# Down products in split 16-bit pairs: a two-FFN and attention kernel on one Trainium2 core

## What is computed

```
x = x + 0.5 * ffn(layernorm(x));  x = x + attn(layernorm(x));  x = x + 0.5 * ffn(layernorm(x))
ffn(x):  scores = sigmoid(x @ router.T); 4 of 16 experts per token, from the best 2 of 4 groups
         h_e = silu(x @ gate_e.T) * (x @ up_e.T)             # 256 -> 128
         y   = sum over chosen e of w_e * (h_e @ down_e.T)   # 128 -> 256
         y  += silu(x @ sh_gate.T) * (x @ sh_up.T) @ sh_down.T   # two shared experts of 128
attn(x): q, k = softplus(gelu(x @ w1.T + b1) @ w2.T + b2); v, g = gelu(x @ w.T + b)
         linear attention over 16 heads (k.T q first), then * z * g, then @ p_w.T + p_b
```

## Time and profile before

| | us |
|---|---|
| median of three runs | 1950.2 |
| the profiled execution | 1945.92 |
| its span, first to last instruction | 1944.2 |
| TensorE busy | 1629.1 (84%) |
| TensorE weight loads | 1253.8 (64%) |
| GpSimd busy | 1115.1 (57%) |
| VectorE busy | 1031.3 (53%) |
| ScalarE busy | 923.8 (48%) |
| mean granted clock of TensorE | 0.943 of 2.4 GHz |

### The profile page before, as it was taken

The page is one execution under the profiler, slowest core; times in us unless marked ns, Lnnn a source line. Parts: engine busy times, 40 slices in busy tenths (PEclk is TensorE's granted clock), DMA queues, the critical chain, the costliest instruction groups (busy, mean ns, idle before and its releaser), DMA issues.

```text
span 1944.2 us, 36213 instructions
## 1 busy us (share of the span) xinstructions
PE 1629.1 (84%) x11159; PEld 1253.8 (64%) x11159; DVE 1031.3 (53%) x3186; ACT 923.8 (48%) x1435; POOL 1115.1 (57%) x1249
## 2 busy tenths in 40 slices
PE   5679999979989999999999999996999998887100
PEld 4447776757777777777777777774777676665100
DVE  4775747634455456557547456556646655232323
ACT  5334443424666556565665656654656642232000
POOL 2677757777033644554454564465466677454676
PEclk9889999999999999999999999999999999999555
DMA  9839998999646855775785785663598799999453
GB/s 311 323 133 249 262 246 245 257 252 258 156 112 168 211 139 146 199 202 146 196 197 153 173 216 155 168 188 87 123 240 212 200 258 289 254 259 296 133 164 118
DMA packets 586145, 393.48 MB, mean 202 GB/s; under 512 B 396375, under 2 KB 547054, under 8 KB 585966
## 3 DMA queue, kind: packets, MB, share of 16 engines
q1 hardware_dynamic: 536626, 256.85, 53.6%
q0 software_dynamic: 49152, 134.28, 22.7%
q10 hardware_dynamic: 188, 0.03, 0.0%
HBM read 101.61 MB, written 197.13 MB: 154 GB/s over the span
## 4 chain that ended last, share of the span: by engine, by line
PE 47%; POOL 20%; DVE 11%; issue 10%; SPq 5%; DMA 5%; ACT 3%; POOLq 0%; DVEq 0%; ACTq 0%
POOL xd L1320 11%; PE bank L993 10%; POOL yg L1334 8%; PE bank L848 6%; PE bank L850 6%; PE bank L849 6%; PE bank L1035 5%; SPq L829 3%; PE bank L997 3%; DVE xb L1547 2%; DMA yg<-yd,idx 2%; DMA xtp<-xd 2%; PE bank L1096 2%; PE bank L937 2%; PE bank L938 2%
## 5 line engine op out<-in xcount | busy, mean ns | idle before, releaser
L1320 POOL DMA_INDIRECT xd<-xs,idx x512 | 517.5, 1011 | 421.9 <-DVE picked L1471 216.4
L1334 POOL DMA_INDIRECT yg<-yd,idx x512 | 505.7, 988 | 231.4 <-issue 152.3
L993 PE MATMUL bank<-dn,h 128*128 x1408 | 377.6, 392 | 57.8 <-ACT ybuf L1190 26.9
L848 PE MATMUL bank<-xtp,gu_hi 128*128 128x256 f16 x1408 | 387.4, 275 | 28.9 <-DMA xtp<-xd 13.5
L1190 ACT ACTIVATE ybuf<-bank 128x512 f32<-128x512 f32 x352 | 209.5, 595 | 389.8 <-PE bank L993 381.4
L849 PE MATMUL bank<-xtp,gu_hi 128*128 128x256 f16 x1408 | 387.0, 275 | 0.0
L850 PE MATMUL bank<-xtp,gu_lo 128*128 128x256 f16 x1408 | 386.8, 275 | 0.0
L1522 DVE SCALAR_TENSOR_TENSOR h<-bank,h 128x512 f32<-128x512 f32 x240 | 165.6, 690 | 321.5 <-PE bank L850 265.5
L993 PEld LDWEIGHTS bank<-dn,h 128*128 128x128 f32 x1408 | 251.3, 194 | 111.5 <-issue 77.9
L1547 DVE SCALAR_TENSOR_TENSOR xb<-yg,comb,xb 128x256 f32<-128x256 f32 x512 | 208.2, 478 | 164.7 <-DMA yg<-yd,idx 164.6
L1183 ACT ACTIVATE h<-bank 128x512 f32<-128x512 f32 x240 | 141.6, 595 | 215.0 <-PE bank L850 126.3
(11 more groups left out here) (191 smaller groups left out, 2527.5 us busy)
## 6 DMA issues: line engine op xcount, KB each, us to landing
yd<-ybuf SPq DMA_DIRECT2D x352, 256.0 KB
xr<-xb SPq DMA_DIRECT2D x32, 512.0 KB, 4.7
xb<-xr SPq DMA_DIRECT2D x32, 512.0 KB
xd<-yg SPq DMA_DIRECT2D x3, 4096.0 KB, 14.6
xb<-in_attn_x_dram SPq DMA_DIRECT2D x16, 512.0 KB
xd<-xs,idx POOLq DMA_INDIRECT x512
yg<-yd,idx POOLq DMA_INDIRECT x512
out_dram<-xb SPq DMA_DIRECT2D x16, 512.0 KB, 3.3
```

Source lines behind the costliest of these rows:

```text
L848: pe.matmul(out_ap, a_hi, b_hi, start=(i == 0), stop=False)
L993: last = pe.matmul(dst, h[:, g % RING_H, c], w, start=True, stop=True)
L1320: pool.indirect_dma_start(out=xd[q % NC][:, :], out_offset=bass.IndirectOffsetOnAxis(ap=idx[:, r % SEQS, t, k:k + 1], axis=0), in_=xs[:, r ...
L1334: pool.indirect_dma_start(out=yg[:, half, t % 2, j].bitcast(U32), out_offset=None, in_=yd[q % NC][:, :], in_offset=bass.IndirectOffsetOnAx ...
```

## The change

The down products are made of 16-bit pairs, as gate and up are, three products each. For that the down weights are split when they are loaded (`dn_hi`, `dn_lo`), and h is split in every unit: silu writes a float32 buffer `m32` (a ring of two), prod multiplies in place with a scale of 8, a new ScalarE piece `h_hi` copies it to 16 bits, a new VectorE piece `h_lo` subtracts, and down waits for `h_lo`. The factor 8 is taken out in the weights of the experts and in the shared sum. The y ring shrinks from eight to seven. The two bias matmuls of the output projection become one, with the high part of the bias in row 0 and the low part in row 32 of one tile. The plan's weights follow: down 0.69 for 0.89, out 4.0 for 4.4, and 0.62 and 0.69 for the two new pieces.

```diff
-RING_Y = 8
+RING_Y = 7
 RING_H = 3
+RING_M = 2
+H_SCALE = 8.0
...
-        ... down=0.89, ... out=4.4),
+        ... down=0.69, ... out=4.0),
+        ACT: h_hi=0.62   DVE: h_lo=0.69   RANK: h_hi=0, h_lo=0
...
-        piece("silu", g, ("gate", g), *[freed] * (g >= RING_H))
+        piece("silu", g, ("gate", g), *[("h_lo", g - RING_M)] * (g >= RING_M))
         piece("prod", g, ("up", g), ("silu", g))
+        piece("h_hi", g, ("prod", g), *[freed] * (g >= RING_H))
+        piece("h_lo", g, ("h_hi", g))
-            piece("down", (g, b), ("prod", g), *before, *[("down", (g, 0))] * b)
+            piece("down", (g, b), ("h_lo", g), *before, *[("down", (g, 0))] * b)
...
-        split = [kind in ("gu", "at") for kind, _ in groups]
+        split = [kind in ("gu", "at", "dn") for kind, _ in groups]
-        dn = sb("dn", [P, NE, D])
+        dn_hi = sb("dn_hi", [P, NE, D], F16)
+        dn_lo = sb("dn_lo", [P, NE, D], F16)
-        h = sb("h", [P, RING_H, TOK])
+        m32 = sb("m32", [P, RING_M, TOK])
+        h = sb("h", [P, RING_H, 2, TOK], F16)
...
             def down(key):
-                pe.wait_ge(prod_done, g + 1)
+                pe.wait_ge(h_lo_done, g + 1)
-                        last = pe.matmul(dst, h[:, g % RING_H, c], w, start=True, stop=True)
+                        last = three(dst, [(h[:, g % RING_H, 0, c], h[:, g % RING_H, 1, c], w_hi, w_lo)])
...
-                    pe.matmul(dst, row0_16[:], pb_hi[:], start=False, stop=False)
-                    last = pe.matmul(dst, row0_16[:], pb_lo[:], start=False, stop=True)
+                    last = pe.matmul(dst, rows16[:], pb[:], start=False, stop=True)
...
             def silu(g):
                 act.wait_ge(gate_done, g + 1)
-                if g >= RING_H:
-                    act.wait_ge(down_done, nth(*plan.h_freed_by[g - RING_H]) + 1)
-                act.activation(h[:, g % RING_H], gate_ps[g % GATES][:], ACT.Silu, scale=INV_W).then_inc(silu_done, 1)
+                if g >= RING_M:
+                    act.wait_ge(h_lo_done, g - RING_M + 1)
+                act.activation(m32[:, g % RING_M], gate_ps[g % GATES][:], ACT.Silu, scale=INV_W).then_inc(silu_done, 1)
+            def h_hi(g):
+                act.wait_ge(prod_done, g + 1)
+                if g >= RING_H:
+                    act.wait_ge(down_done, nth(*plan.h_freed_by[g - RING_H]) + 1)
+                act.activation(h[:, g % RING_H, 0], m32[:, g % RING_M], ACT.Copy).then_inc(h_hi_done, 1)
...
+            def h_lo(g):
+                dve.wait_ge(h_hi_done, g + 1)
+                dve.tensor_tensor(h[:, g % RING_H, 1], m32[:, g % RING_M], h[:, g % RING_H, 0], ALU.subtract).then_inc(h_lo_done, 1)
```

More of the change, by code:

```diff
@@ L57 @@
 TABLE_STEPS = 14
-CONSTS = 29
+CONSTS = 30
 def stages():
@@ L81 @@
         SP=dict(wload=0.5, load=0.5, store=0.5, zero_rows=1.0, xload=2.6, ystore=0.5),
-        PE=dict(turn_w=0.5, small=0.4, turnR=0.95, logits=0.75, rank=0.25, turn_tab=0.3, gate=1.36, up=1.36, down=0.89,
-                turnA=0.95, proj=2.65, second=3.5, gproj=1.36, kv=1.85, z=0.5, apply=1.85, regroup=0.95, out=4.4),
+        PE=dict(turn_w=0.5, small=0.4, turnR=0.95, logits=0.75, rank=0.25, turn_tab=0.3, gate=1.36, up=1.36, down=0.69,
+                turnA=0.95, proj=2.65, second=3.5, gproj=1.36, kv=1.85, z=0.5, apply=1.85, regroup=0.95, out=4.0),
         ACT=dict(small_hi=0.6, w_hi=0.6, w_copy=0.6, norm=2.1, normA=2.1, xs_hi=1.05, xtf_hi=1.03, xtf_lo=1.03, sigmoid=0.9,
-                 silu=0.62, yev=0.62, xta_hi=1.2, gelu=2.0, absolute=1.05, exp=2.1, ln=2.1, gate_gelu=1.9, ot=1.6),
+                 silu=0.62, h_hi=0.62, yev=0.62, xta_hi=1.2, gelu=2.0, absolute=1.05, exp=2.1, ln=2.1, gate_gelu=1.9, ot=1.6),
         POOL=dict(rootR=1.7, rootA=1.7, scatter=5.1, gather=5.1),
         DVE=dict(small_lo=0.6, w_lo=0.69, group_p=0.5, stats=1.85, xs_lo=1.25, scores=0.8, groups=1.85, experts=2.3,
-                 slots=1.5, weights=2.2, table_cols=3.7, table=0.3, prod=0.7, shared_sum=0.7, combine=3.3,
+                 slots=1.5, weights=2.2, table_cols=3.7, table=0.3, prod=0.7, h_lo=0.69, shared_sum=0.7, combine=3.3,
                  statsA=1.85, xta_lo=1.4, add_bias=1.4, gate_bias=0.7, finish=1.25,
@@ L92 @@
     TABLE = dict(sigmoid=("exp", "gelu", "silu"), silu=("silu",), gelu=("gelu",), gate_gelu=("gelu",), exp=("exp",), ln=("ln",))
-    RANK = dict(down=0, silu=0, yev=0, prod=0, rootR=0, rootA=0)
+    RANK = dict(down=0, silu=0, yev=0, prod=0, h_hi=0, h_lo=0, rootR=0, rootA=0)
     EARLY = ("stats", "norm", "xs_hi", "xs_lo", "turnR", "xtf_hi", "xtf_lo", "logits", "sigmoid", "scores", "groups",
@@ L309, in unit_for @@
         r, p = self.next_shared, self.next_pair
-        if r < 2 * SEQS and ("xtf_lo", r) in self.ended and ("xtf_hi", r) in self.ended and ("w_copy", 2) in self.ended:
-            best = max(at, self.ended["xtf_lo", r], self.ended["xtf_hi", r], self.ended["w_copy", 2]), ("shared", r, 0)
-        if p < self.pairs and ("xload", p) in self.ended and ("w_copy", self.n_ffn - 1) in self.ended:
-            start = max(at, self.ended["xload", p], self.ended["w_copy", self.n_ffn - 1])
+        if r < 2 * SEQS and ("xtf_lo", r) in self.ended and ("xtf_hi", r) in self.ended and ("w_lo", 2) in self.ended:
+            best = max(at, self.ended["xtf_lo", r], self.ended["xtf_hi", r], self.ended["w_lo", 2]), ("shared", r, 0)
+        if p < self.pairs and ("xload", p) in self.ended and ("w_lo", self.n_ffn - 1) in self.ended:
+            start = max(at, self.ended["xload", p], self.ended["w_lo", self.n_ffn - 1])
             if best is None or start < best[0]:
@@ L766, in _ @@
                 sp.dma_start(row_bias[:, i, :], b.partition_broadcast(P)).then_inc(rows_loaded, 16)
-            sp.dma_start(pb_row, p_b.rearrange("(o d) -> o d", o=1)).then_inc(rows_loaded, 16)
+            for row in pb_rows:
+                sp.dma_start(row, p_b.rearrange("(o d) -> o d", o=1)).then_inc(rows_loaded, 16)
             def wload(n):
@@ L991, in down @@
                         c = slice(b * SLOT + j * P, b * SLOT + (j + 1) * P)
-                        w = dn[:, bass.ds(e, 1), :].rearrange("p e o -> p (e o)")
-                        last = pe.matmul(dst, h[:, g % RING_H, c], w, start=True, stop=True)
+                        w_hi, w_lo = (w[:, bass.ds(e, 1), :].rearrange("p e o -> p (e o)") for w in (dn_hi, dn_lo))
+                        last = three(dst, [(h[:, g % RING_H, 0, c], h[:, g % RING_H, 1, c], w_hi, w_lo)])
                     else:
                         c = slice((2 * b + j) * P, (2 * b + j + 1) * P)
-                        for s in range(SHARED):
-                            last = pe.matmul(dst, h[:, (g - 1 + s) % RING_H, c], dn[:, E + s, :],
-                                             start=(s == 0), stop=(s == SHARED - 1))
+                        parts = [h[:, (g - 1 + s) % RING_H] for s in range(SHARED)]
+                        last = three(dst, [(part[:, 0, c], part[:, 1, c], dn_hi[:, E + s], dn_lo[:, E + s])
+                                           for s, part in enumerate(parts)])
                 last.then_inc(down_done, 1)
@@ L1241, in _ @@
             plan.walk(dict(small_hi=small_hi, w_hi=w_hi, w_copy=w_copy, norm=norm, normA=normA, xs_hi=xs_hi, xtf_hi=xtf_hi,
-                           xtf_lo=xtf_lo, sigmoid=sigmoid, silu=silu, yev=yev, xta_hi=xta_hi, gelu=gelu,
+                           xtf_lo=xtf_lo, sigmoid=sigmoid, silu=silu, h_hi=h_hi, yev=yev, xta_hi=xta_hi, gelu=gelu,
                            absolute=absolute, exp=exp, ln=ln, gate_gelu=gate_gelu, ot=ot_))
@@ L1617, in _ @@
                            scores=scores_, groups=groups_, experts=experts_, slots=slots_, weights=weights_,
-                           table_cols=table_cols, table=table, prod=prod, shared_sum=shared_sum, combine=combine,
+                           table_cols=table_cols, table=table, prod=prod, h_lo=h_lo, shared_sum=shared_sum, combine=combine,
                            add_bias=add_bias, gate_bias=gate_bias, finish=finish_kq, kv_mask=kv_mask, mix=mix,
```

43 lines of the change are left out of this document (24 added, 19 removed).

## The result

The changed kernel takes 1962.6 us (median of 20 runs, 1954.0 to 1976.4), the kernel before 1949.8 (20 runs, 1938.4 to 1960.8). The ratio is **1.0067** with an interval of [1.0047, 1.0087]: 13 us slower, where 1918 us and a gain were forecast. The profiled execution has a span of 1958.1 us, before it was 1944.2.

What follows compares the result with a forecast made beforehand. The prediction took TensorE to bound the kernel between 420 and 1600: 67.1 us saved, less 16 for waits, 9 for GpSimd and 10 at the end, is 32.1, so the median of 1950.2 becomes 1918 us, range 1868 to 1968.

Steps and rivals of the forecast that it cites:

- a cheaper down product pays between 420 and 1600: In 420:1600, where TensorE was taken to set the pace, less down and bias work saves 67.1 us.
- The price of a down: On TensorE, a routed down falls from 0.87 us to 0.66 us, as six 16-bit matmuls.
- The first rival: Attention sequences, 70 us apart, set the pace and TensorE's saving turns idle: 1950 to 1960 us, no change; chance 0.17.
- The sign that the prediction set for it: In the attention stages: the same 70 us between applies, with TensorE busy for less, would show the forecast wrong.
- GpSimd: In 150:420, VectorE's new subtraction holds up scatters: 9 us lost, bounds 0 to 26.
- The passes: Splitting h adds 144 us of work on ScalarE and 166 on VectorE; both have room, so no cost was counted.
- The waits on the pair: TensorE's 23 waits in 420:1600 grow by up to 1.4 us each: between 0 and 32 us, 16 taken.
- The ends: First 150 us: 0 taken, between -16 and +7; last group: combines and gathers slip behind the last pairs, 10 us lost.
- The bias matmul and the y buffers: One bias matmul less in each of 64 cases saves TensorE 7.0 us; seven y buffers cost 0, bounds 0 and 7.1.
- a move by more than 20 us: Last stretch: a shift that large would show the forecast wrong and be the plan's new order, no engine's cost.

Runs made afterwards that it cites:

- e3: Changed kernel's operations without the split of h (the high part stands in for the low), in the order of the kernel before: 1938.8 us, 0.9935 of before.
- e12: Changed operations without the split of h, in exactly the order of e11: 1871.7 us, 0.9593 of the kernel before.
- e13: Changed operations without the split of h, in an order with head starts chosen for them: 1862.3 us, 0.9538 of the kernel before.
- e2: Changed kernel's order, with float32 downs and no split of h, one bias matmul and seven y buffers: 2002.6 us, 1.0266 of the kernel before.
- e6: Changed kernel in its own order, without the split of h and with five h buffers: 1942.7 us, 0.9973 of the kernel before.
- e4: As e3, in the order of the kernel before, but one product per down in place of three: 1922.1 us, 0.9846 of the kernel before.
- e7: As e6, in the changed kernel's order, but both splitting passes run and no down waits for them: 1962.1 us, 1.0072 of the kernel before.
- e10: All operations of the changed kernel, in an order chosen through head starts by kind of piece: 1908.5 us, 0.9762 of the kernel before.
- e14: Kernel before with a separate buffer for attention's normalized input, six y buffers and a chosen order: 1909.3 us, 0.9788 of before.
- e15: As e3, in the order of the kernel before, but VectorE's subtraction alone runs, and no down waits for it: 1958.8 us, 1.0043 of before.
- e1: All operations of the changed kernel, in the order of the kernel before, planned without the new pieces: 2103.1 us, 1.0783 of before.
- e8: Kernel before in its own order, with one bias matmul, seven y buffers and five h buffers: 1954.8 us, 0.9998 of before.
- e9: Kernel before with only the plan's price of a down changed, 0.90 for 0.89, which gives a new order: 1981.0 us, 1.0134 of before.
- e11: Operations of the kernel before, in an order with head starts chosen for them: 1888.2 us, 0.9667 of before.

## Why the prediction was wrong

**The step that failed** is the one that stands alone in its paragraph: "So a cheaper down product pays between 420 and 1600", with its 67.1 us. The price of a down was right (0.66 us). By that price the downs and the bias matmuls make 108 us over the span, and TensorE is 68 us less busy, with its granted clock at 0.916 for 0.943. But as time the saving came back at 13 us in the order of before (e3), 14 in a better one (e12), 25 in one made for it (e13), and in the changed kernel's own order, with the passes away, it leaves 5 us against before (e6). The 57 us from e2 to e6 show that TensorE's work can count, in an order that was made for short downs; the kernel before was not in one. The rows that misled are 679 of 700 us busy and 34 us of waits on h. Both are true, and neither says that others wait for TensorE: in a list that was written out so that TensorE always has something to do, it is busy whether it is late or early. e4 shows what the view of waits cannot: TensorE's busy time falls by 222 us, and 199 of them become its idle time.

**The first rival** had the mechanism: it named attention's pace and 1950 to 1960 us. The sign that the prediction set for it, the same 70 us between applies with TensorE busy for less, came (72.5 us from mix to mix, and 68 us less busy). That its number lies 3 us beside the measurement is luck: its terms were 10 us of waits, 9 of GpSimd and up to 10 at the end, and nothing for the passes, which cost 19 (e7). And it called the 70 us the chain of a sequence, which is not shown: the orders of e10 to e13 have the same chain at 67 to 68, and e14, with one buffer's tie taken out, is at 69.7.

The Trainium skill, in "Perfetto Trace Analysis", "Identifying the Most-Contended Engine", would judge TensorE not by matmul busy time but by its weight loads, beside the FLOPs done. The loads were 535 of 700 us, and e3 and e4 agree with the headroom that this leaves; e2 to e6, from 517 of 700, does not. I had set the page aside for the waits on h.

**The passes** were given room and no price ("ScalarE and VectorE have the room"). They cost 36 us in the old order and 19 in the new, in the old most of it VectorE's 0.69 us per unit (e15), though VectorE was busy 398 of 700 us; some 8 us of that fit GpSimd's longer scatters. This is the second term that was missed, and with the first it makes the sign.

**The waits on the pair**, +16 us: 0 in the changed kernel (e7), 129 without an order that knows of them (e1). That the plan finds other matmuls to put between was the right end of that range. The bound of 1.4 us on each of 23 waits could not have reached the other end, since in e1 there are 61 waits in 420:1600, 125 us in all.

**GpSimd**, +9 us: in 150:420 the mean scatter took 984 ns before and takes 1004, with 179 of them in the stretch, so 3.6 us. The rows of before and of after, in the view of groups over that stretch:

```profile
L1320 POOL DMA_INDIRECT xd<-xs,idx x166 | 163.4, 984 | 64.5 <-issue 48.8 <-DVE picked L1471 14.4 <-DVE beats_ge L1434 0.3
```

```profile
L1337 POOL DMA_INDIRECT xd<-xs,idx x179 | 179.7, 1004 | 62.0 <-issue 54.1 <-DVE idx L1485 5.2 <-DVE picked L1488 1.8
```

A scatter that starts while the subtraction runs is held by it: 19 of the 179 do, and they take 1.17 us on the mean by the timeline, the others 0.96 for the most part. How many do is a matter of the order: in the old one the scatters up to the first mix lost 8.4 us (e15), close to the 9 of the sum, in the changed kernel they take 3.2 us more than before. The inference in "SBUF — State Buffer", "Who interferes with whom" of the Trainium skill, that tensor_tensor does not stall descriptor generation, has against it the scatter of 1.65 us that starts at 300.09, under a subtraction of 1.23 us.

```profile
299.69 1.23 DVE L1415 TENSOR_TENSOR xs<-xn,xs 128x1024 f16<-128x1024 f32 x1
```

```profile
300.09 1.65 POOL L1337 DMA_INDIRECT xd<-xs,idx  x1 [0.30 <-issue]
302.05 0.96 POOL L1337 DMA_INDIRECT xd<-xs,idx  x1 [0.30 <-issue]
```

**The ends**, 0 and +10: the first scatter starts at 68.3 us and started at 54.5. It is at 54.6 in e8, 58.4 in e3, which also splits the down weights, and 67.2 in e6, which has the new order too. So some 4 us go with the weights and 9 with the order. After the last mix the kernel is 29.6 us shorter and not 10 longer; with e9 in mind, such a shift is put down to the order and to no engine, as the prediction said of a move by more than 20 us; no run tests this one.

**The bias matmul and the y buffers**: 7.0 and 0 us were taken, 0 for both came (e8).

In all, for the path by the old order: -13 for TensorE, +36 for the passes, +129 for the chain, -140 from the new order. By the new order: -5 for TensorE and the order together, +19 for the passes, -1 for the chain. Both paths end at the measured +13 by construction, since each step is the difference of two runs; what they show is the size of the steps.

What stays open: which wait, or which set of them, holds the sequences 67 us apart when neither TensorE's work (e12) nor the order nor the buffer of e14 moves them far. And e13 and e11 are not bounds: other orders may be better than those chosen.

## What to carry to other kernels

An engine that is 97% busy in a list that was written out in advance is not shown to be the bound; take most of the work in question away in one run and see what the time does, before counting a saving at full value. Price every added pass by a run in which it works for nobody: 0.7 us per unit on an engine with 40% idle time cost 21 us, a third of the 67 that were counted, and part of that seems to have come through another engine. And where a planner writes the order, move one of its prices by a hundredth first: what the time does then (1.3% in the one trial here) is the least that a change must show before it is credited or blamed, and the order itself may hold more (3.3%) than the operations.

## What was not expected of the hardware

TensorE's granted clock fell where TensorE had more idle time. In 1650:1700 TensorE was 39.8 of 50 us busy before, and is 17.1 after; the granted clock is 0.93 and 0.65 of 2.4 GHz, means over stretches at its levels of 2.4 and 1.2 GHz. The first row is of before, the second of after:

```profile
1650.00:1700.00 50.00, 39.82 (x242) 29.82 (x241) 11.77 (x24) 14.93 (x25) 22.16 (x23) 0.93 1.10 253
```

```profile
1650.00:1700.00 50.00, 17.10 (x105) 10.31 (x102) 26.97 (x98) 6.54 (x11) 34.50 (x35) 0.65 0.60 194
```

This gap is the order's and not the saving's: the second stretch holds most of one wait of 33.7 us for a load of the last group, and e2, with the old operations in the same order, has such a wait of 34.7. The view of waits in 1600:1720 of after:

```profile
PE bank L859 <- DMA xtp<-xd: 41.0, 6, 33.7
```

Where the work is nearly the same, in 600:1300, the clock is 1.00 before, 0.98 in e3 and 0.95 in e4. Over the span it is 0.943 before, 0.916 after and 0.884 in e4, the run with the least work for TensorE. So part of a saving on TensorE may be taken back by slower matmuls; how much of the time that is here was not measured by itself.
